# Transposing the input of a fused two-layer kernel: from TensorE and ScalarE to VectorE, on squares loaded in transposed places

## What is computed

```python
def reference(...):
    x = L0_attn_hidden_states                       # (32, 256, 128)
    x = _layernorm(x + _L0_attn_ref(x, Wq, Wk, Wv, Wg, Wo, lepe_w, lepe_b))   # part a
    x = _layernorm(x + _L0_ffn_ref(x, W, Wp, bp, sim, temp, Wd0, Wu0, ...))   # part b
    x = _layernorm(x + _L1_attn_ref(x, W, b))                                 # part c
    x = _layernorm(x + _L1_ffn_ref(x, w_gate, w1_e, w3_e, w2_e, ...))         # parts r, d
    return x

# part a: q, k, v and a gate are products of x with 128x128 weights
q = (hidden_states @ Wq.T).reshape(Bb, Ss, H, DK)
k = (hidden_states @ Wk.T).reshape(Bb, Ss, H, DK)
v = (hidden_states @ Wv.T).reshape(Bb, Ss, H, DV)
o_gate = hidden_states @ Wg.T
o = mala_attn(q, k, v) + lepe_conv(v, lepe_w, lepe_b)
return (o * o_gate) @ Wo.T
# the last feed-forward: a gate picks 4 of 16 experts for each row; their weights are "combine"
routed = jnp.einsum('tef,ehf,te->th', g * u, w2_e, combine)
```

## Time and profile before

| | |
|---|---|
| runs of the kernel before | 723.78, 725.48, 726.61 us; median 725.48 |
| span of the profiled execution | 722.4 us |
| busy: TensorE, VectorE, ScalarE, GpSimd | 659.3, 587.1, 486.4, 309.0 us |
| TensorE's starts of turns 9, 10, 11, 12 | 342.46, 382.26, 422.76, 462.56 us |

### The profile page before, as it was taken

The page is one execution under the profiler, slowest core; times in us unless marked ns, Lnnn a source line. Parts: engine busy times, 40 slices in busy tenths (PEclk is TensorE's granted clock), DMA queues, the critical chain, the costliest instruction groups (busy, mean ns, idle before and its releaser), DMA issues.

```text
span 722.4 us, 13085 instructions
## 1 busy us (share of the span) xinstructions
PE 659.3 (91%) x3654; PEld 508.6 (70%) x3654; DVE 587.1 (81%) x1873; ACT 486.4 (67%) x978; POOL 309.0 (43%) x793
## 2 busy tenths in 40 slices
PE   3466679999999999999999999999999999999994
PEld 2354557787878777777878787777868787767652
DVE  1566778989898898889898898889897998877672
ACT  2243548587786878686877877686877868676623
POOL 1234443445453535536454535436454535340311
PEclk9787979999999999999999999999999999999997
DMA  6000000000000010101000000101000000000001
GB/s 226 12 4 15 1 16 0 16 1 16 15 15 15 1 30 2 31 0 29 0 15 16 5 25 0 30 0 29 0 21 9 15 0 0 15 1 15 16 0 30
DMA packets 18678, 12.51 MB, mean 17 GB/s; under 512 B 704, under 2 KB 18240, under 8 KB 18368
## 3 DMA queue, kind: packets, MB, share of 16 engines
q1 hardware_dynamic: 18624, 11.95, 5.5%
HBM read 7.75 MB, written 4.19 MB: 17 GB/s over the span
## 4 chain that ended last, share of the span: by engine, by line
PE 68%; DVE 14%; ACT 7%; issue 6%; POOL 3%; DMA 1%; DVEq 0%; ACTq 0%; SPq 0%; POOLq 0%
PE bank L556 13%; PE bank L351 8%; PE bank L353 8%; PE bank L352 8%; PE bank L360 8%; PE bank L439 2%; PE bank L466 2%; PE bank L411 2%; PE bank L454 2%; DVE conv L954 2%; DVE gu L1067 1%; PE bank L477 1%; PE bank L510 1%; PE bank L478 1%; PE bank L523 1%
## 5 line engine op out<-in xcount | busy, mean ns | idle before, releaser
L556 PE MATMUL bank<-hid,whole 128*128 128x512 f32 x288 | 147.2, 593 | 0.8 <-DVE hid L1070 0.8
L351 PE MATMUL bank<-x3T_hi,w_hi 128*128 128x512 f32 x288 | 138.2, 480 | 1.8 <-DVE gu L1067 1.4
L738 ACT ACTIVATE silu<-bank 128x512 f32<-128x512 f32 x144 | 86.4, 600 | 65.0 <-PE bank L353 61.9
L1067 DVE TENSOR_TENSOR gu<-silu,bank 128x512 f32<-128x512 f32 x128 | 86.7, 677 | 41.1 <-ACT silu L738 18.5
L353 PE MATMUL bank<-x3T_hi,w_lo 128*128 128x512 f32 x288 | 113.5, 394 | 0.0
L352 PE MATMUL bank<-x3T_lo,w_hi 128*128 128x512 f32 x288 | 112.7, 391 | 0.0
L1171 POOL TENSOR_TENSOR moment<-stats 128x4 f32<-128x4 f32 x192 | 44.8, 266 | 150.1 <-DVE stats L881 134.3
L1077 DVE TENSOR_TENSOR hid<-gu,bank 128x512 f32<-128x512 f32 x128 | 87.2, 681 | 1.8 <-PE bank L556 0.8
L351 PEld LDWEIGHTS bank<-x3T_hi,w_hi 128*128 128x128 f32 x288 | 54.2, 188 | 31.0 <-ACT silu L738 9.9
L1157 POOL TENSOR_TENSOR qk<-rope_c,rope_s 128x512 f32<-128x512 f32 x32 | 40.6, 1280 | 82.6 <-DVE rope_s L843 82.6
L1171 POOL TENSOR_TENSOR rstd<-moment,whole 128x4 f32<-128x4 f32 x64 | 64.7, 1011 | 5.0
(11 more groups left out here) (196 smaller groups left out, 1635.7 us busy)
## 6 DMA issues: line engine op xcount, KB each, us to landing
x_in<-x SPq DMA_DIRECT2D x16, 256.0 KB, 2.9
out<-x SPq DMA_DIRECT2D x16, 256.0 KB, 2.3
whole<-w_whole SPq DMA_DIRECT2D x1, 1198.5 KB, 5.7
w_raw<-w SPq DMA_DIRECT2D x1, 1152.0 KB
w_raw<-w SPq DMA_DIRECT2D x1, 546.0 KB, 7.0
whole<-w_whole SPq DMA_DIRECT2D x16, 32.0 KB
whole<-w_whole SPq DMA_DIRECT2D x1, 64.0 KB
```

What stands on the lines that cost most here:

```text
L351: mm(out, wh, mh, start=True, stop=False)
L556: mm(YB[:], whole[:, a:a + P], hid[:, c % 2], start=c == 0, stop=c == CHUNKS).then_inc(p_w2.sem, 1)
L738: fn(silu[:, c % 2], GB[:], ACT.Silu).then_inc(a_silu.sem, 1)
L1067: tt(gu[:, c % 2], silu[:, c % 2], UB[:], ALU.mult).then_inc(v_gu.sem, 1)
```

## The change

The input is loaded a second time, into a new tile `x_sq` [128, 2, 512]. Four DMAs of 32 partitions fill a half of it. Seen as 32x32 squares, the square of rows q and features j lands where the square (j, q) of the transposed block belongs, not transposed in itself. One VectorE `transpose` of 128x512 then transposes each 32x32 square in its place, and writes `xT[0]` in SBUF. TensorE's `a_xT_` and the wait in front of it are gone, and so is ScalarE's second copy; x0T_hi is now made from `xT[0]`. The wait for `v_mix` moves to the first matmul that writes A0, in `a_qk`. ScalarE's `x0_hi` waits for the transpose and for TensorE's last use of x0T_hi (`p_g` of the block before). VectorE transposes block i+1 near the end of turn i, behind `a_res`, ahead of `r_combine`; block 0 in front of turn 0. It waits for the squares and for GpSimd having read the block before (`g_x0l`). VectorE's loop now has four iterations, and its turns 14 and 15 are written out; the other engines' loops keep five.

```diff
+    sq_view = x_dram.rearrange("(n q p) (j c) -> n j p q c", q=BLOCK // SQUARE, p=SQUARE, c=SQUARE)
...
+            def load_squares(n, half):
+                for j in range(P // SQUARE):
+                    nc.sync.dma_start(x_sq[j * SQUARE:(j + 1) * SQUARE, half].rearrange("p (q c) -> p q c", c=SQUARE),
+                                      sq_view[n, j]).then_inc(sq_ld[half].sem, 16)
...
             def load_after(n, half):
+                sp.wait_ge(v_sq.sem, v_sq.at(n))
+                load_squares(n + 2, half)
                 sp.wait_ge(v_res[0].sem, v_res[0].at(n))
                 nc.sync.dma_start(x_in[:, half], x_view[n + 2]).then_inc(x_ld[half].sem, 16)
...
-            def a_xT_(n, half, load):
-                pe.wait_ge(x_ld[half].sem, x_ld[half].at(load))
-                if started(n):
-                    pe.wait_ge(v_mix.sem, v_mix.at(n - 1))
-                transpose_tiles(A0, lambda t: x_in[:, half, t], ident).then_inc(p_xT[0].sem, 1)
...
             def x0_hi(n):
-                act.wait_ge(p_xT[0].sem, p_xT[0].at(n))
-                fn(x0T_hi[:], A0[:], ACT.Copy).then_inc(a_x0h.sem, 1)
-                fn(xT[0][:], A0[:], ACT.Copy).then_inc(a_xT[0].sem, 1)
+                act.wait_ge(v_sq.sem, v_sq.at(n))
+                if started(n):
+                    act.wait_ge(p_g.sem, p_g.at(n - 1))
+                fn(x0T_hi[:], xT[0][:], ACT.Copy).then_inc(a_x0h.sem, 1)
...
+            def a_square(n, half, load):
+                dve.wait_ge(sq_ld[half].sem, sq_ld[half].at(load))
+                if started(n):
+                    dve.wait_ge(g_x0l.sem, g_x0l.at(n - 1))
+                nc.vector.transpose(xT[0][:], x_sq[:, half]).then_inc(v_sq.sem, 1)
...
-                if a: a_res(i, odd)
+                if a: a_res(i, odd, load)
+                if not last(i): a_square(i + 1, 1 - odd, next_load)
                 if c: r_combine(i - 2)
...
-            with dve.Fori(0, loops) as k:
-                turn(2 * k + LEAD, 0)
-                turn(2 * k + LEAD + 1, 1)
+            with dve.Fori(0, loops - 1) as k:
+                turn(2 * k + LEAD, 0, k + LEAD // 2, k + LEAD // 2)
+                turn(2 * k + LEAD + 1, 1, k + LEAD // 2, k + LEAD // 2 + 1)
+            for i in range(blocks - 2, blocks):
+                turn(i, i % 2, i // 2, (i + 1) // 2)
```

More of the change, by code:

```diff
@@ L42 @@
 SUB = 32
+SQUARE = 32
 EXPERTS, GROUPS, EF = 16, 4, 64
@@ L117, in build, with last @@
     assert blocks % 2 == 0 and loops > 0
+    def last(n):
+        return isinstance(n, int) and n >= blocks - 1
     def live(n):
         return not isinstance(n, int) or 0 <= n < blocks
+    sq_view = x_dram.rearrange("(n q p) (j c) -> n j p q c", q=BLOCK // SQUARE, p=SQUARE, c=SQUARE)
     x_view = x_dram.rearrange("(n t p) d -> n p t d", t=TILES, p=P)
@@ L182, in build @@
         x_in = sb("x_in", [P, 2, TILES, P])
+        x_sq = sb("x_sq", [P, 2, BLOCK])
         xT = [sb(f"x{k}T", [P, BLOCK]) for k in range(4)]
@@ L276, in build @@
         x_ld = [sig(f"x_ld{i}", 16) for i in range(2)]
+        sq_ld = [sig(f"sq_ld{i}", 16 * (P // SQUARE)) for i in range(2)]
         setup_v, setup_a, setup_p, setup_g = sig("setup_v"), sig("setup_a"), sig("setup_p"), sig("setup_g")
-        p_xT = [sig(f"p_x{k}T") for k in range(4)]
-        a_xT = [sig(f"a_x{k}T") for k in range(4)]
+        v_sq = sig("v_sq")
+        p_xT = {k: sig(f"p_x{k}T") for k in (1, 2, 3)}
+        a_xT = {k: sig(f"a_x{k}T") for k in (1, 2, 3)}
         a_x0h, g_x0l, a_x3h, g_x3l = sig("a_x0h"), sig("g_x0l"), sig("a_x3h"), sig("g_x3l")
@@ L310, in _ @@
         def _(sp):
+            def load_squares(n, half):
+                for j in range(P // SQUARE):
+                    nc.sync.dma_start(x_sq[j * SQUARE:(j + 1) * SQUARE, half].rearrange("p (q c) -> p q c", c=SQUARE),
+                                      sq_view[n, j]).then_inc(sq_ld[half].sem, 16)
             nc.sync.dma_start(whole[:, C_LATE:], whole_dram[:, C_LATE:]).then_inc(k_in.sem, 16)
+            load_squares(0, 0)
+            nc.sync.dma_start(w_raw[:, W_LATE:], weight_dram[:, W_LATE:]).then_inc(w_in.sem, 16)
             nc.sync.dma_start(x_in[:, 0], x_view[0]).then_inc(x_ld[0].sem, 16)
-            nc.sync.dma_start(w_raw[:, W_LATE:], weight_dram[:, W_LATE:]).then_inc(w_in.sem, 16)
+            load_squares(1, 1)
             nc.sync.dma_start(x_in[:, 1], x_view[1]).then_inc(x_ld[1].sem, 16)
@@ L391, in a_qk @@
                 for h, b in ((0, A0), (1, A1)):
+                    if h == 0 and started(n):
+                        pe.wait_ge(v_mix.sem, v_mix.at(n - 1))
                     if h == 1:
@@ L560, in d_yT, with turn @@
                 transpose_tiles(YB, lambda t: tile(yT, t), ident).then_inc(p_yT.sem, 1)
-            def turn(i, odd, load=None):
+            def turn(i, odd):
                 a, b, c, d, e = live(i), live(i - 1), live(i - 2), live(i - 3), live(i - 4)
-                if a: a_xT_(i, odd, load)
                 if d: d_hidden(i - 3, 1 - odd, 0)
@@ L607, in _ @@
             for i in range(LEAD):
-                turn(i, i % 2, i // 2)
+                turn(i, i % 2)
             with pe.Fori(0, loops) as k:
-                turn(2 * k + LEAD, 0, k + LEAD // 2)
-                turn(2 * k + LEAD + 1, 1, k + LEAD // 2)
+                turn(2 * k + LEAD, 0)
+                turn(2 * k + LEAD + 1, 1)
             for i in range(blocks, turns):
@@ L887, in a_layer_norm, with a_res @@
                        ALU.subtract, ALU.mult).then_inc(v_x1.sem, 1)
-            def a_res(n, half):
+            def a_res(n, half, load):
+                dve.wait_ge(x_ld[half].sem, x_ld[half].at(load))
                 dve.wait_ge(p_y.sem, p_y.at(n))
@@ L1084, in d_res, with turn @@
                 norm_stats(3, n)
-            def turn(i, odd):
+            def turn(i, odd, load=None, next_load=None):
                 a, b, c, d, e = live(i), live(i - 1), live(i - 2), live(i - 3), live(i - 4)
+                if not started(i): a_square(0, 0, 0)
                 if d: d_gu(i - 3, 0)
@@ L1134, in _ @@
             for i in range(LEAD):
-                turn(i, i % 2)
-            with dve.Fori(0, loops) as k:
-                turn(2 * k + LEAD, 0)
-                turn(2 * k + LEAD + 1, 1)
+                turn(i, i % 2, i // 2, (i + 1) // 2)
[3 more added lines that the diff above has]
+            for i in range(blocks - 2, blocks):
+                turn(i, i % 2, i // 2, (i + 1) // 2)
             for i in range(blocks, turns):
@@ L1194, in x0_lo @@
                 pool.wait_ge(a_x0h.sem, a_x0h.at(n))
-                pool.wait_ge(a_xT[0].sem, a_xT[0].at(n))
                 tt(x0T_lo[:], xT[0][:], x0T_hi[:].bitcast(F32), ALU.subtract).then_inc(g_x0l.sem, 1)
```

## The result

| | median | runs | ratio to before, 95% interval |
|---|---|---|---|
| before, on the same chip | 725.24 us (723.78 to 726.61) | 7 | |
| after | 727.20 us (726.69 to 728.02) | 7 | 1.003 (1.0021 to 1.0039) |

The change costs 2.0 us, 0.3%: clear of the scatter, but within the 0.5% that the prediction called no change. The profiled execution spans 725.4 us, 3.0 more than the one of before. The profiled execution of after took 727.20 us, exactly the median, 1.8 above its span; in all runs recorded with both, the time lies 1.75 to 1.94 us above the span. That the spans differ by 3.0 and the medians by 2.0 then comes from a fast execution before, not from the change.

The account below looks back on a forecast made before the run. TensorE bounds the steady turn, with a loop through VectorE's `comb` only 0.44 us shorter; +2.5 +0.65 +0.6 -0.6 +0.2 = +3.3 us on the 725.5 median gave 728.8, range 723 to 736.

Parts of the forecast that it names:

- same: Whole kernel: change within about 0.5% (3.6 us), chance 0.50; faster 0.08, slower 0.42.
- start, to the first matmul on x0T: From setup to first matmul on x0T: shorter chain -1.1, squares queued ahead of weights +1.3, in all +0.2 us.
- back edges: VectorE's loop jump: one stop fewer, -0.7 us; three left lose 0.44 us of slack each, +1.3; together +0.6.
- Two cycles, the second takes over: Steady turn: VectorE's path through `comb`, TensorE and ScalarE (40.01 us) overtakes TensorE's own work (39.44); turn +0.21 us.
- T: VectorE's added transpose ahead of `comb`: 0.65 us, range 0.3 to 1.2; total change 13T - 5.1 us.
- Rival 4: VectorE's transpose is cheap, T of 0.3 to 0.5: -1.2 to +1.4 us, no tellable change; chance 0.15.
- Rival 1: VectorE's transpose takes more than one plain pass, up to two: +10.5 us, 736.0; chance 0.36 for T above 0.67.
- the room: Steady turn before: the loop through `comb` is 0.44 us shorter than TensorE's own work, 39.36 against 39.80.
- TensorE gives back 0.36 a turn: Start of each turn: dropping four x_in transposes frees TensorE 0.36 us, at most 4.7 us over turns 3 to 15.
- ScalarE's copy counted as nothing: Before softmax: dropping a 128x512 copy gains nothing, as softmax waits for VectorE's maxima; otherwise up to -0.5 us a turn.
- Packets of 128 bytes: Squares' load on SP's queue: 17 ns a packet taken, between 7 and 27; 2.2 us ahead of the weights.
- Rival 2: Start: a 128-byte packet costs 54 ns, squares hold the weights 6.0 us instead of 1.3: 733.5; chance 0.06.

Follow-up runs that it names:

- the mid-turn version: Kernel after with VectorE's transpose moved ahead of the third d_gu, where VectorE waited for Silu: 721.06 us, 0.9947 of the kernel before.
- the last experiment: Kernel after with the transpose in mid turn, the weights loaded first and VectorE's loop written out: 714.39 us, 0.9862 of the kernel before.

## Why the prediction was right, and where its sizes were off

**Time, range and sign.** 728.8 was forecast, 727.2 measured, with "same" the likeliest of the three. The forecast took +3.3 us, the median rose by 2.0 and the profiled span by 3.0. The mechanism was right; the sum is close because errors of opposite sign cancel. By the two traces its terms measure, in us:

| term | forecast | measured |
|---|---|---|
| start, to the first matmul on x0T | +0.2 | +0.63 |
| from there to the end of turn 1 | 0 | +0.44 |
| from there to `a_vT_` of turn 2 | -0.6 | -0.95 |
| from there to `comb` of turn 3 | +0.65 | +0.76 |
| turns 4 to 15 as plain turns | +2.5 | +1.73 |
| back edges | +0.6 | +0.29 |
| length of turn 3 | 0 | +0.13 |
| sum | +3.3 | +3.03 |

**Two cycles, the second takes over: shown.** Taking TensorE's work back in changed nothing; half a transpose and two moved the turn one for one; moving the transpose out of the second cycle gave the gain. All signs that the prediction named are there: a VectorE row of 0.70 between statistics and MAX8, the wait for `comb`, plain turns of 40.00, three long ones of 41.12 to 41.16 (forecast 41.1), first matmul at 15.51. The recorded stop is 0.38 to 0.55 us in turns 4 to 15 and not 0.57, since the matmul ahead of it is counted until it has run out; by the pitch of 0.23 between such matmuls `comb`'s transposes could have begun at 345.51 + 0.23 = 345.74, and 0.62 is lost.

**T = 0.65: nearly.** The transpose moves MAX8 by 0.63; from the third `gu` to `comb` VectorE takes 25.41 us, 24.73 before, so T is 0.68 with its waits. 256 columns took 427 ns, 512 took 692: 1.04 ns a column and 0.16 us fixed. By the Trainium skill, Vector Engine (DVE) Microarchitecture Reference, section 3.8, one element per cycle per lane gave the estimate of 0.53 us for streaming; these rows agree with it (512 × 1.04 ns = 0.53 us). Rival 4 needed T under 0.5 and is out. Rival 1 needed T above 0.67, and 0.68 is above it: by the prediction's own 13T - 5.1 that is +3.7 us, "slower" by a hair. That the kernel is nonetheless the same within 0.5% is due to the room, which the prediction had too small, and to the back edges, which it had too dear (both below), so on that side its "same" was luck. What rival 1 said in words, a transpose dearer than one plain pass, is not so: it takes 0.69 us, as the plain pass of the earlier trace rows does.

**TensorE gives back 0.36 a turn: too little.** With the x_in transposes `d_hidden` starts 1.25 us after the last matmuls of the turn before (L483) begin, 341.57 to 342.82; without them 0.80 (in the mid-turn version 340.85 to 341.65). It is 0.45.

**ScalarE's copy counted as nothing: the step that failed.** The prediction said "the softmax waits for VectorE's maxima anyway", and took it as nothing because TensorE showed no stop. TensorE didn't stop by a row's reckoning, but its second matmul on probT stood 0.33 us behind the first instead of 0.22. Turn 9 before, then after:

```profile
351.12 0.49 PE L510 MATMUL bank<-cv,probT 128*128 128x128 f32 x2
351.45 0.39 PE L511 MATMUL bank<-cv,probT 128*128 128x128 f32 x2
```

```profile
353.22 0.39 PE L525 MATMUL bank<-cv,probT 128*128 128x128 f32 x2
353.44 0.39 PE L526 MATMUL bank<-cv,probT 128*128 128x128 f32 x2
```

With the copy back in the mid-turn version the wider pitch is back too (0.32, from 352.88 to 353.20). ScalarE was a third cycle, on the softmax, and it was worth 0.13 a turn. Thus TensorE's own cycle is 39.80 - 0.45 - 0.13 = 39.22 with the change, 39.25 as the last experiment measured it; the forecast was 39.44. And the room of the second cycle was not 0.44 but 0.47 to 0.56: `comb`'s 0.69, 0.55 to 0.64 to the scores, 9.70, 3.57 to the third `gu`, and 24.73 make 39.24 to 39.33. Most of the difference is the same 0.13, since the scores' stretch is part of both cycles, and in the prediction's 39.36 it is the stretch of before, 9.83. T was a little larger and the room too, which is why plain turns still came out near the forecast of +0.21: +0.15 to +0.24 in the loop, but only +0.06 and +0.12 in the written-out turns 4 and 5, where VectorE takes 25.35 and not 25.41 us to `comb`, and -0.07 in turn 15.

**The back edge: +0.3 instead of +0.6.** Its turns were 3.1 us longer than plain ones, now 3.4 (3 × 1.12 to 1.16). The forecast for after was right (3 × 1.14); that for before was from turn 9 to 10 alone, 0.70, where turn 12 had 0.94.

**From `comb` in turn 3 to `comb` in turn 16** the two traces differ by +2.15 us, against +3.1 forecast. Taken at the plain turns' change, turns 4 to 15 give 1.7 and not 2.5 (+0.20 where there is a back edge, +0.04 in turn 14, which has none now), the edges 0.3 and not 0.6, and turn 3's length 0.1.

**Up to turn 3: +0.88 in the traces** (104.76 to 105.64), against +0.65 - 0.6 + 0.2 = +0.25 forecast. At the start the first matmul came +0.63, and not +0.2. The weights were held 1.43 (forecast 1.3), but the chain behind them gave back 0.8 and not 1.1: its passes are as forecast (0.71, 0.63, 1.26), its four hand-overs take 0.08 to 0.15 each, where 0.06 was taken for three. After that the two executions differ by TensorE's granted clock, a term that the prediction did not have. In turns 0 and 1 it changes between its two levels, 0.50 (1.2 GHz) and 1.00 (2.4 GHz). In turn 1, before and then after:

```profile
43.00:45.20 2.20, 2.08 (x16) 1.71 (x15) 1.73 (x5) 0.60 (x1) 1.65 (x2) 1.00 0.01 4
43.00:45.20 2.20, 2.20 (x12) 2.20 (x11) 2.10 (x5) 0.83 (x2) 0.67 (x1) 0.50 0.00 0
```

The first matmul on x0T of turn 1 begins at 39.15 before and at 40.13 after, each behind more than 5 us of idle time of TensorE. From there its matmuls of 256 columns are 0.21 us apart; the pitch falls to 0.12 at 42.3 before, while after it stays at 0.21 to the last of them, at 43.95. So the lag grows from 0.98 us to 1.74 at `b_small` (44.33 against 46.07). In turn 0 it is likewise: the four transposes of `att` take 0.68 us before and 1.10 after. Later in turn 1 it is the other way round, 1.11 before and 0.66 after, and at the turn's end the lag is 1.07 (61.89 against 62.96). From there to `a_vT_` of turn 2 it falls by 0.95 to 0.12. Of this, 0.42 are four matmuls of the output weights (L477 and L478 before), 3.02 us before (63.60 to 66.62) and 2.60 after, the second pair alone 1.32 and 0.94; 0.53 are left for what the prediction put at 0.6. Whether the change shifts these steps of the clock, or chance does, isn't shown. Executions of one kernel differ too: of the kernel with the transpose in mid turn one took 719.2 us at a mean granted clock of 0.972, another 722.1 at 0.962. From 60 to 100 us the traces of all these kernels show mean granted clocks between 0.76 and 0.84 (0.80 both before and after), from 200 us on full.

**Packets of 128 bytes: 13 ns, not 17.** In a window of 9 us with one store, one load of squares and one of x_in, the kernel after has on its queue:

```profile
q1 hardware_dynamic: 3168, 0.79, 39.2%
```

39.2% of 16 engines over 9 us is 56.4 us; less 1,056 packets at 27 ns, 2,112 small ones took 27.9 us, 13 ns each. Rival 2 is out. The start gives nearly the same: the weights landed at 8.7 us before, at 10.2 after, and at 8.4 with the squares behind them, so the squares held them 1.8 us (14 ns for each of 128 packets), where the prediction said 2.2, and x_in, moved behind them, gave back 0.3, where it said 0.9. The two errors nearly cancel in its +1.3. The Trainium skill, DMA: Bandwidth & Descriptors, first table, names 512 bytes as the least for line rate; here bytes per time do fall by half, but a small packet costs less than a large one, and nothing of the loads shows in a steady turn. The prediction's "no transfer of the trace was of that kind" holds for loads and stores only: the page before counts 704 packets under 512 bytes, that of after 34,496, which is 16 more for each of the 64 added loads, beside their 32,768.

## What to carry to other kernels

Ask of an added instruction not how long it is but which cycle it lands in: 0.7 us of VectorE cost 0.2 us a turn ahead of `comb` and nothing in front of a wait that was there anyway, in the same kernel with the same work. Before crediting a saving on the busiest engine, work out every cycle that closes over it with its room, for the saving ends where the next cycle begins; and look at the pitch of its matmuls too, since a late partner can cost a tenth of a microsecond without a recorded stop. A bound should be tested by putting the removed work back: if the time doesn't move, the removal bought nothing in that kernel. In the mid-turn version, where the second cycle has its room again, plain turns did fall by 0.5 us.

## What the runs showed that I had not expected

- VectorE's loop stops it 1.8 us at each back edge, with nothing to wait for. That cost 0.7 to 1.2 us of the turn (up to 1.4 in the mid-turn version). In turn 10 before, the softmax waits 0.70 us for the maxima and TensorE 0.47 for probT; writing one engine's loop out gave 0.5% without any other edit.
- An fp32 STREAM_TRANSPOSE of 128x512 in SBUF takes 0.69 us, as an elementwise pass of that size does, while four fp32 transposes of 128x128 hold TensorE 0.36 to 0.45.
- SP's issue of the weights' load took 2.37 us behind four loads with 512 packets each; the second load of w_raw, in the same kernel, took 0.50.
